# Layer norms from accumulated sums and squares, another order of the last two tiles, and tile quantisation on VectorE

## The reference

```
a   = x + LN(Attention(LN(x)))
out = a + LN(FFN(LN(a)))
LN(v) = (v - mean) / sqrt(var + 1e-5)
Attention: 32 query heads, 8 key/value heads, head size 128, causal softmax, output projection to 512 columns
FFN(v) = Q(silu(Q(v) W1^T) * (Q(v) W3^T)) W2^T, inner size 1792
Q(v): for each row and each block of 128 columns, scale = max|v| / 448 + 1e-12, then (v / scale) * scale
```

## Time and profile before

| | |
|---|---|
| median of the runs | 1239.38 us |
| profiled execution, its own time | 1240.05 us |
| its span, first to last instruction | 1238.3 us |
| TensorE matmul busy | 1206.2 us, 97% |
| VectorE busy | 781.8 us, 63% |
| ScalarE busy | 604.3 us, 49% |
| GpSimd busy | 692.1 us, 56% |
| mean granted TensorE clock | 0.994 |

### The profile page before, as it was taken

The page is one execution under the profiler, slowest core; times in us unless marked ns, Lnnn a source line. Parts: engine busy times, 40 slices in busy tenths (PEclk is TensorE's granted clock), DMA queues, the critical chain, the costliest instruction groups (busy, mean ns, idle before and its releaser), DMA issues. The chain is left out here.

```text
span 1238.3 us, 18359 instructions
## 1 busy us (share of the span) xinstructions
PE 1206.2 (97%) x6188; PEld 1001.9 (81%) x6188; DVE 781.8 (63%) x1945; ACT 604.3 (49%) x1365; POOL 692.1 (56%) x827
## 2 busy tenths in 40 slices
PE   8999999999999999999999999999998899999996
PEld 7788888878888888888888888888876677888885
DVE  4544544466666666666766666766678765655568
ACT  6433243256656666566666656657567521111111
POOL 7745455433725635546535536528456687766645
PEclk9999999999999999999999999999999999999998
DMA  6534553341131131131131221311410111011101
GB/s 215 147 151 170 188 203 137 136 136 18 31 90 26 27 85 27 26 94 22 28 89 26 67 53 22 94 23 30 141 18 1 52 39 49 18 49 51 51 0 68
DMA packets 160834, 89.76 MB, mean 72 GB/s; under 512 B 137584, under 2 KB 145776, under 8 KB 157424
## 3 DMA queue, kind: packets, MB, share of 16 engines
q1 hardware_dynamic: 160752, 88.72, 24.8%
HBM read 61.43 MB, written 27.26 MB: 72 GB/s over the span
## 5 line engine op out<-in xcount | busy, mean ns | idle before, releaser
L465 POOL TENSOR_SCALAR probs_long<-probs_long,rsum 128x928 f32<-128x928 f32 (+15 forms) x128 | 119.4, 933 | 259.0 <-DVE rsum L896 258.3
L832 DVE TENSOR_TENSOR pT_lo<-psT,pT_hi 128x512 fp32r<-128x512 f32 (+3 forms) x384 | 211.7, 553 | 79.8 <-ACT pT_hi L686 77.2
L686 ACT CAST pT_hi<-psT 128x512 fp32r<-128x512 f32 (+3 forms) x384 | 182.3, 476 | 68.9 <-PE psT L1211 67.0
L1115 PE MATMUL psS<-kT_hi,qT_hi 128*128 128x256 f32 (+8 forms) x384 | 148.1, 386 | 0.0
L1211 PE MATMUL psT<-ident,probs_long 128*128 128x128 f32 x832 | 136.0, 277 | 8.1 <-DVE pT_lo L832 6.9
L1211 PEld LDWEIGHTS psT<-ident,probs_long 128*128 128x128 f32 x832 | 102.0, 141 | 48.4 <-DVE pT_lo L832 31.5
L691 ACT ACTIVATE probs_long<-probs_long,negmax 128x928 f32<-128x928 f32 (+15 forms) x128 | 122.2, 954 | 38.0 <-DVE negmax L888 37.7
L1115 PE MATMUL psS<-kT_hi,qT_lo 128*128 128x256 f32 (+8 forms) x384 | 127.5, 332 | 0.0
L1115 PE MATMUL psS<-kT_lo,qT_hi 128*128 128x256 f32 (+8 forms) x384 | 127.0, 331 | 0.0
L888 DVE CUSTOM_DVE_ANT_0 probs_long<-psS,mask 128x928 f32<-128x928 f32 (+15 forms) x128 | 123.9, 968 | 3.9 <-PE psS L1115 2.2
L1227 PE MATMUL psOY<-pT_hi,v_hi 128*128 128x512 f32 x288 | 118.7, 412 | 2.3 <-DVE pT_lo L832 2.2
(11 more groups left out here) (150 smaller groups left out, 2955.2 us busy)
## 6 DMA issues: line engine op xcount, KB each, us to landing
q_raw<-q_scr SPq DMA_DIRECT2D x256, 64.0 KB, 2.3
raw<-in_w_qk SPq DMA_DIRECT2D x10, 1024.0 KB, 5.8
q_scr<-cB SPq DMA_DIRECT2D x16, 512.0 KB, 2.6
q_scr<-cA SPq DMA_DIRECT2D x16, 512.0 KB, 2.6
raw_wd<-in_w_dense SPq DMA_DIRECT2D x8, 1024.0 KB, 7.6
raw_up<-in_w_up SPq DMA_DIRECT2D x7, 1024.0 KB, 4.8
v_scr<-vout SPq DMA_DIRECT2D x16, 256.0 KB, 2.4
kT_lo<-k_scr SPq DMA_DIRECT2D x8, 512.0 KB, 4.2
```

Source lines behind the costliest of these rows:

```text
L465: nc.gpsimd.tensor_scalar(row, row, rsum[:, h:h + 1], 1.0, ALU.mult, ALU.mult).then_inc(p_ready, 1)
L686: nc.scalar.copy(dst, src).then_inc(t_hi, 1)
L832: return nc.vector.tensor_tensor(dst, source, hi.bitcast(F32), ALU.subtract)
L1115: last = nc.tensor.matmul(dst, a, b, start=(start and k == 0), stop=(stop and k == len(terms) - 1), skip_group_check=resumed)
```

## The change

- The addition of a tile of `y` in the last group also accumulates its row sum (`add_projection`). Two 128x1 operations make the negative mean and a bias from it (`sum_y`). For x the mean is known from the first norm; the norm before has mean zero, so the mean of the sum is that of x (`means`, once).
- ScalarE squares the centred tile into a scratch tile and accumulates the variance (`square`). GpSimd makes the root. VectorE makes the offset, mean times root, 128x1. ScalarE normalises in one pass (scale and bias). The residual moves from VectorE to GpSimd.
- `tile_scales` goes on to quantise the tile on VectorE: four operations on 128x128, SBUF to SBUF.
- The last two steps are exchanged: tile 4 is step 6, tile 0 is step 7. Tile 4 gets a buffer of its own (`probs_mid`), since two long tiles now follow each other.
- The stages stand in explicit places (a table by step, and lists written out for the first FFN chunk). The first tile's transpose ("X", 0) moves into the last attention step, the weights W one or more steps earlier. The first chunk's `down` result is copied out of PSUM by ScalarE instead of VectorE.
- TensorE's order in the first chunk is gate_up(n-1), transpose of tile n, down(n-3), turn_hidden(n-2).

More of the change, by code:

```diff
@@ L93, in step_items @@
                 items.append(("RKV", g + 1, (s - 4) * 2 + h // 2))
-            if last:
-                items += [(kind, s - lag) for kind, lag in NORMS[h] if s >= lag]
+            if last and s in NORMS:
+                items += NORMS[s][0][h]
         if two:
@@ new lines, in _ @@
+                elif kind == "X":
+                    lo_of_xn1(*args)
+                elif kind == "means":
+                    nc.vector.tensor_scalar(xmean[:], mv[:, :, 0], -1.0, None, ALU.mult)
+                    nc.vector.tensor_scalar(xbias[:], mv[:, :, 0], -D ** -0.5, (EPS / D) ** 0.5, ALU.mult,
+                                            ALU.add).then_inc(mean_x, 1)
+                elif kind in ("sum_y", "offset_y", "offset_x1", "scales"):
+                    norms(kind, *args)
@@ new lines, in _ @@
+            norms("offset_x1", 3)
+            norms("offset_y", 4)
+            norms("scales", 2)
+            norms("offset_y", 5)
+            make_hidden(0, 0)
+            lo_of_xn1(1)
+            norms("scales", 3)
+            add_projection(T - 1)
+            norms("sum_y", 7)
+            norms("offset_x1", 4)
+            norms("offset_y", 6)
+            make_hidden(1, 1)
+            lo_of_xn1(2)
+            norms("offset_x1", 5)
+            lo_of_hidden(0, 0)
+            norms("scales", 4)
@@ new lines, in _ @@
+            make_hidden(2, 0)
+            lo_of_xn1(3)
+            norms("offset_y", 7)
+            norms("offset_x1", 6)
+            lo_of_hidden(1, 1)
+            norms("scales", 5)
+            make_hidden(3, 1)
+            lo_of_xn1(4)
+            lo_of_hidden(2, 0)
+            norms("scales", 6)
+            for n in range(5, NT + 1):
+                make_hidden(n - 1, (n - 1) % 2)
+                if n < NT:
+                    lo_of_xn1(n)
+                    if n >= NT - 2:
+                        link(nc.vector.memset(y[:, LAST[n], :], 0.0))
+                if n == 5:
+                    norms("offset_x1", 7)
+                lo_of_hidden(n - 2, n % 2)
+                if n == 5:
+                    norms("scales", 7)
@@ L1209, in turn_probs @@
                 bank = psT[:, turn % 2, :]
-                for j in range(b * TPB, min((b + 1) * TPB, ORDER[t % NT] + 1)):
+                for j in range(b * TPB, min((b + 1) * TPB, TILES[t] + 1)):
                     last = nc.tensor.transpose(bank[:, (j % TPB) * P:(j % TPB + 1) * P],
```

359 lines of the change are left out of this document (199 added, 160 removed).

## The result

The changed kernel takes 1245.47 us (median of six runs, 1243.49 to 1247.72), the kernel before 1239.28 on the same chip: ratio 1.0045, 95% interval 1.003 to 1.006. It is slower, by 6.2 us. The profiled execution, the longest of the six, took 1247.72 us with a mean granted clock of 0.989 (the other five had 0.991 to 0.993); against 1240.05 of the one before that is +7.67.

What follows compares the result with a forecast made beforehand. TensorE, busy 97% of the span, was the bound. g8 at 964.6 + 47.3 + 1.2 = 1013.1 against 1015.15, with -0.45 behind it, gave -2.5: 1237.5 from the profiled 1240.05, 1236.8 as median; range 1229 to 1246.

Steps and rivals of the forecast that it cites:

- The attention: Steps 3 to 7 of the last group: 7.7 us won, PV of step 7 ending at 964.6 against 972.27.
- A: Stretch from the start of step 3 to the end of the last PV; its steps 5 to 7 forecast at 31.9 us.
- the cadence of gate_ups 1 to 7: First FFN chunk, times between gate_up starts; 7.5 us for 2 to 3, from VectorE's offset waiting for GpSimd's root.
- my port term: First FFN chunk: VectorE's quantisations held up by GpSimd operations at the shared ports; 1.2 us in all, bounds 0 and 10.
- B: Stretch from the end of the last PV to g8, gate_up 8's start; forecast 47.3 us plus 1.2 for ports.
- within my case, +1.9: Rival without its own chance: the clock falls again after a 1.5 to 2 us wait in step 7 or the chunk.
- The lost lead: First FFN chunk: tiles no longer transposed a gate_up ahead; each gate_up from the third waits 0.7 us, 5.45 a tile.
- The products on VectorE: Four 128x128 quantisations a tile, moved from GpSimd to VectorE: 0.8 us for the four, waits apart.
- VectorE becomes the bound: Rival, chance 0.20: in the first chunk each VectorE quantisation takes turns with a GpSimd operation; +9 us, 1245.
- Places that fit: Rival, chance 0.30: roots and residuals ready; steps 3, 5 and 6 lose under 1 us, 7.5 becomes 5.4; 1230.5 us.
- Another table for the squares: Rival, chance 0.04: squares need another table than silu; five pairs of loads in the chunk, some 8 us; 1244.
- Behind g8: After gate_up 8 starts: chunk 2's weights in time for GpSimd, -0.45 us on TensorE; the rest unchanged.

Runs made afterwards that it cites:

- e2: Changed kernel with each tile's turn, high part and low part issued one product earlier again, as in the kernel before: 1238.8 us.
- e6: Kernel of e2 with the norm chain reordered on VectorE, GpSimd and ScalarE, so ready steps stand ahead of waiting ones: 1234.0 us.
- e3: Changed kernel with 26, 34 and 14 transposes of the identity ahead of gate_up 2, 4 and 6: 1240.3 us.
- e4: Kernel before with only the lead taken away: turn, high part and low part of tile n issued in pass n: 1245.7 us.
- e7: Kernel of e6 with the products that quantise tiles 2 to 7 on GpSimd again: 1236.6 us.
- e12: Kernel of e6 without the four products a tile by which VectorE quantises the tiles: 1231.2 us.
- e8: Kernel of e6 with GpSimd's preparation of the second chunk's weights begun one tile later: 1237.5 us.
- e1: Changed kernel without the four products a tile by which VectorE quantises the last group's tiles: 1235.9 us.
- e9: Kernel of e6 with VectorE's low part of tile 2 in front of the addition of the last projection: 1234.4 us.

## Why the prediction was wrong

Forecast was 1236.8 us, 2.5 faster; the kernel became 6.2 slower. Term by term:

- *The attention*: right. A was to be 55.5 us and is 55.98; steps 3 and 4 took 15.15 and 8.98 (14.54 and 8.99 forecast), steps 5 to 7 31.85 (31.9). In step 3 TensorE waits 2.2 us for low parts (a loss of 2.1 forecast), and ScalarE 0.38 for a residual. PV of step 7 ended at 965.3 (964.6).
- *The first terms of the chunk*: right. First wait 0.97 (1.0), g0 to g1 6.58 (6.6), g7 to g8 4.36 (4.4).
- *The step that failed* is the cadence of gate_ups 1 to 7: "5.4; 2 to 3: 7.5; 3 to 4: 5.9; then three times 5.5". It was 6.77, 7.87, 10.02, 7.83, 6.87 and 6.98: 46.34 against 35.3, 11.0 more, of which my port term had 1.2. It failed in two ways. I set durations of rows one behind the other and took each engine's inputs as present; but the norms of the last tiles were placed behind silus, so each delay of TensorE came back through ScalarE, GpSimd's roots and VectorE's offsets. Nothing but places mends this: B is 58.25 in the changed kernel, 49.59 with the lead restored (e2) and 45.65 with the other places too (e6; they were not tried without the lead). And I kept the clock "within my case, +1.9": it fell three times, and e3 has it at 5.6 us of B.
- *The lost lead*: seen, but priced at 4.4 us for the chunk (47.3 against 42.9) with everything else in it. Alone it costs 6.6 of B (e4).
- *The products on VectorE*: I took 0.8 us for four, they take 1.11 where GpSimd leaves them alone. With GpSimd they took 2.16, 1.84, 1.11, 3.14, 2.35 and 1.11 for tiles 2 to 7, 5.0 over that; three block scales took 1.15, 1.09 and 0.94 instead of 0.17, 2.7 over. That is 7.7 us of turns on VectorE, where I put 1.2 on the path. The Trainium skill, "SBUF — State Buffer", section "SBUF: two separate sides", has a VectorE operation on both read ports, or with two SBUF inputs against a GpSimd operation that reads SBUF, and that operation exclude each other for a whole instruction. The trace agrees: 3.14 us beside GpSimd's 0.65, 1.27 and 1.26, which were not lengthened themselves.
- *The rival "VectorE becomes the bound"* gave 1245, the very number, and its condition held (7.7 us of turns over six tiles, 1.3 a tile). The agreement is in part luck, for its mechanism is half of the truth. Leaving the products out gave 9.6 us, restoring the lead 6.7, filling the waits 5.1: 21.4 us together, where B had 9.8 us more than forecast. The three aren't terms of a sum. They feed the same waits, and whichever goes first takes the slow gate_ups with it. VectorE was busy only 25.54 of 38 us; its queue was late, not full. In e6 the products stay, and nothing is gained by GpSimd having them (e7); leaving them out altogether gives 2.8 (e12).
- *Places that fit*: didn't come. *Another table for the squares*: no load of a table stands between the squares and silu but the one before the first silu.
- *Behind g8*: right. -0.45 forecast, -0.60 found; GpSimd no longer waits for chunk 2's weights.

What stays open: how much of e12's 4.6 us in B is the products' own time and how much their turns; behind which waits the clock falls; and why the part in front of step 3 differs by up to 2.6 us between traces of programs that are alike there.

## What to carry to other kernels

When a change makes a wait on a helper engine, put every step whose data is there ahead of any step in the same queue that waits for TensorE or for another helper; otherwise the delay runs round the loop and grows. Look for a lead that the edit takes away, and count it alone: here it was worth 6.1 us (e4) to 6.7 (e2), nearly all of the seven that the change won in the attention. Don't add up what single cures bring while they act on the same wait, and price a TensorE wait of microseconds with the slow products that can follow it. Before work on a helper is moved later, look at what its end releases: in e8 it was the next load of weights, and the delay came out one chunk further on.

## What the hardware showed that I had not expected

- Behind waits of 3.09, 4.09 and 1.81 us (changed kernel) and 3.08 (e4) TensorE's products ran at 1.2 GHz and cost 1.6 to 2.3 us more per gate_up; 26 idle transposes in 3.00 us in the place of the wait kept it at 2.4 GHz (e3). But not every such wait did it: behind 2.40 us in e2, 2.30 in e7, 1.97 in e3, 1.84 in e12 and 1.73 in e1 no product ran at 1.2 GHz.
- A smaller wait is no safe one, nor a sure one: in e6 0.70 and 0.97 us, with four transposes between, stood ahead of a gate_up of 4.43 us; in e2 0.74 and 0.98, with the same four between, ahead of one of 2.90; in e9 the wait of 0.74 alone, of 2.86.
- VectorE's four 128x128 products took 1.11 us alone, 1.12 beside a 128x1 root of GpSimd (which took 0.69 there instead of 0.55), and as long as GpSimd's operations beside 128x512 ones (3.14, 3.26).
